# A router's product with the high and low part of its weights side by side, in a decoder layer on one core

## The reference

```python
x = x + attention(layernorm(x))
x = x + convolution(layernorm(x))
h = layernorm(x).reshape(-1, 256)
router_logits = h @ gate_w.T                    # 16 experts
routing_probs = softmax(router_logits)
topk_w, topk_idx = top_k(routing_probs, 4)
topk_w = topk_w / topk_w.sum(-1, keepdims=True)
shared = silu_mul(h @ shared_gate_up.T) @ shared_down.T
shared = shared * sigmoid(h @ shared_gate_vec.T)
x = x + shared + (each expert's output, weighted with topk_w where it is chosen)
```

## Time and profile before

| | |
|---|---|
| median of three runs | 956.32 us |
| the runs | 954.98 to 961.11 us |
| span of the profiled execution | 957.6 us |
| instructions | 19531 |
| mean granted clock of TensorE | 0.989 of 2.4 GHz |
| busy: TensorE, VectorE, GpSimd, ScalarE | 96%, 81%, 53%, 46% |

### The profile page before, as it was taken

How to read it: one execution, slowest core, us unless ns; L and a number is a source line. 1 busy time by engine, 2 the same in 40 slices (tenths; PEclk the granted TensorE clock), 3 DMA queues, 4 the chain that set the end, 5 groups by cost and what they waited for, 6 DMA issues and landing times.

```text
span 957.6 us, 19531 instructions
## 1 busy us (share of the span) xinstructions
PE 919.9 (96%) x6337; PEld 825.6 (86%) x6337; DVE 771.4 (81%) x1704; ACT 439.1 (46%) x1227; POOL 505.0 (53%) x380
## 2 busy tenths in 40 slices
PE   6899999999999999999999999989999999999996
PEld 6789898989899888989888898877887799999985
DVE  6978877977887989877798976765778888888857
ACT  3656745454434654333564333472245444444430
POOL 1453424465453435777453677624626377777760
PEclk9999999999999999999999999998999999999998
DMA  7786389899156952303793231325151277787769
GB/s 267 260 339 238 131 305 388 313 393 364 53 181 246 400 191 105 111 24 117 287 373 115 88 112 48 122 65 237 52 216 69 75 126 130 129 132 129 125 109 314
DMA packets 75586, 179.09 MB, mean 187 GB/s; under 512 B 7777, under 2 KB 42465, under 8 KB 74465
## 3 DMA queue, kind: packets, MB, share of 16 engines
q1 hardware_dynamic: 61040, 158.80, 46.0%
q0 software_dynamic: 14448, 19.05, 12.2%
HBM read 98.35 MB, written 79.47 MB: 186 GB/s over the span
## 4 chain that ended last, share of the span: by engine, by line
PE 76%; DVE 8%; issue 6%; DMA 3%; POOL 3%; ACT 2%; SPq 1%; another core or an unknown queue 0%; DVEq 0%; POOLq 0%; ACTq 0%
PE bank L550 11%; PE bank L552 10%; PE bank L551 10%; PE bank L852 6%; PE bank L630 6%; PE bank L954 3%; POOL xs L1350 3%; PE bank L830 3%; PE bank L616 3%; PE bank L832 3%; PE bank L834 3%; PE bank L656 3%; PE bank L658 2%; PE bank L657 2%; DVE turn L1514 2%
## 5 line engine op out<-in xcount | busy, mean ns | idle before, releaser
L1310 POOL TENSOR_TENSOR z_lo<-prob_t,z_hi 128x512 fp32r<-128x512 f32 x64 | 82.5, 1296 | 191.3 <-ACT z_hi L1197 167.6
L1514 DVE SCALAR_TENSOR_TENSOR turn<-bank,bqk,trig 128x1024 f32<-128x1024 f32 x128 | 160.6, 1277 | 23.3 <-PE bank L552 20.8
L1342 POOL TENSOR_TENSOR rot<-turn 128x512 f32<-128x512 f32 x64 | 101.8, 1591 | 107.4 <-DVE turn L1514 91.9
L1403 POOL DMA_INDIRECT sums<-ysb,token_at x79 | 123.3, 1561 | 57.0 <-DMA sums<-ysb,token_at 26.4
L550 PE MATMUL bank<-xt_hi,w_hi 128*128 128x512 f32 x256 | 105.4, 412 | 3.1 <-DVE xt_lo L1478 1.7
L1183 ACT COPY prob_t<-bank 128x512 f32<-128x512 f32 x64 | 37.5, 586 | 150.9 <-PE bank L616 142.7
L1142 ACT ACTIVATE prob<-prob,negmax 128x128 f32<-128x128 f32 x256 | 99.1, 389 | 2.5 <-DVE negmax L1499 2.4
L552 PE MATMUL bank<-xt_hi,w_lo 128*128 128x512 f32 x256 | 100.0, 391 | 0.0
L551 PE MATMUL bank<-xt_lo,w_hi 128*128 128x512 f32 x256 | 99.7, 390 | 0.0
L1350 POOL DMA_INDIRECT xs<-xh,dest x64 | 71.8, 1122 | 41.9 <-issue 38.3
L1153 ACT COPY v<-bank 128x512 f32<-128x512 f32 x64 | 37.6, 588 | 119.7 <-PE bank L552 118.6
(11 more groups left out here) (201 smaller groups left out, 2663.9 us busy)
## 6 DMA issues: line engine op xcount, KB each, us to landing
xs<-zeros SPq DMA_DIRECT2D x16, 2120.0 KB, 15.6
w_hi<-w_dram SPq DMA_DIRECT2D x24, 768.0 KB, 10.0
w_lo<-w_dram SPq DMA_DIRECT2D x24, 768.0 KB, 9.4
xe_all<-xs SPq DMA_DIRECT2D x79, 132.5 KB
wo_hi<-wo_dram SPq DMA_DIRECT2D x26, 256.0 KB, 9.6
wo_lo<-wo_dram SPq DMA_DIRECT2D x26, 256.0 KB, 11.1
sums<-zeros SPq DMA_DIRECT2D x3, 2176.0 KB, 13.0
raw<-in_wqkv SPq DMA_DIRECT2D x16, 384.0 KB, 4.4
```

Source lines behind the costliest of these rows:

```text
L1342: nc.gpsimd.tensor_tensor(rot[m][1][:], turn[m][1], turn[m][2], ALU.add).then_inc(rot_pool, 1)
L1403: nc.gpsimd.indirect_dma_start(sums_dram[s % SUMS], bass.IndirectOffsetOnAxis(ap=token_at[:, s:s + 1], axis=0), ysb[s % YBUFS][:], None, c ...
L1514: last = nc.vector.scalar_tensor_tensor(turn_all[m][:, 2 * i:2 * i + 2, :], qk_bank[2 * m + i][:].unsqueeze(1).to_broadcast([128, 2, GT]), ...
```

## The change

`gate_hi` and `gate_lo` become the two halves of one tile `gate_both` (36 columns for each half of the features). `token_logits` multiplies the high part and the low part of a block each once with all 36 columns; the sum over both parts and both halves of the features stands in 36 columns of PSUM: what was multiplied with the weights' high part, and beside it what was multiplied with their low part. The product low x low, which was left out before, is now in it. `logits_take` adds the two halves while it moves them to SBUF, with a reduction in place of the copy. A group uses 144 columns of the bank in place of 72. 24 matmuls of 18 columns become 16 of 36. Nothing is moved in any queue.

```diff
         gate = sb("gate", [128, CH, LG])
-        gate_hi = sb("gate_hi", [128, CH, LG], F32R)
-        gate_lo = sb("gate_lo", [128, CH, LG], F32R)
+        gate_both = sb("gate_both", [128, CH, 2 * LG], F32R)
+        gate_hi, gate_lo = gate_both[:, :, 0:LG], gate_both[:, :, LG:2 * LG]
...
                 for b in range(GB):
                     t = slice(b * 128, (b + 1) * 128)
-                    last = product3_at(o[:, b * LG:(b + 1) * LG],
-                                       [(hi[:, c, t], lo[:, c, t], gate_hi[:, c, :], gate_lo[:, c, :])
-                                        for c in range(CH)], b)
+                    for c in range(CH):
+                        for part in (hi, lo):
+                            last = nc.tensor.matmul(o[:, b * 2 * LG:(b + 1) * 2 * LG], part[:, c, t], gate_both[:, c, :],
+                                                    start=(b == 0 and c == 0 and part is hi),
+                                                    stop=(c == CH - 1 and part is lo), skip_group_check=True)
                 last.then_inc(logit_ready, 1)
...
-                    nc.scalar.copy(gate_hi[:], gate[:]).then_inc(gate_hi_done, 1)
+                    nc.scalar.copy(gate_hi, gate[:]).then_inc(gate_hi_done, 1)
...
-                nc.vector.tensor_copy(logit[:, bs, :], bank[:, 0:GB * LG].rearrange("p (b e) -> p b e", b=GB)).then_inc(logit_taken, 1)
+                both = bank[:, 0:GB * 2 * LG].rearrange("p (b h e) -> p b e h", b=GB, h=2)
+                nc.vector.tensor_reduce(logit[:, bs, :], both, AX.X, ALU.add).then_inc(logit_taken, 1)
...
-                    nc.vector.tensor_tensor(gate_lo[:], gate[:], gate_hi[:].bitcast(F32), ALU.subtract).then_inc(gate_lo_done, 1)
+                    nc.vector.tensor_tensor(gate_lo, gate[:], gate_hi.bitcast(F32), ALU.subtract).then_inc(gate_lo_done, 1)
```

## The result

The changed kernel takes 952.98 us (median of 9 executions, 950.46 to 958.89), the kernel before 960.72 in the same series (9 executions, 953.73 to 962.56). The ratio is 0.9938, 95% interval 0.9911 to 0.9966: faster by 0.6%, which is within the 1% called no change. It is taken over all the executions; the two medians alone would give 0.992, since those of nine executions that spread over 8 to 9 us are uncertain by about a microsecond each. The forecast of 950.9 against 956.32 is a ratio of 0.9943.

What follows compares the result with a forecast made beforehand. TensorE, 96% busy, was taken as the bound. -1.78 (groups 0, 1) + 0.12 (group 2) - 0.77 (group 3) - 1.49 - 1.5 (clock) = -5.4 us, from the median of 956.3 to 950.9 us; range 947.0 to 956.5.

Steps and rivals of the forecast that it cites:

- Pitch and run: In each of four places, 16 matmuls start 0.112 us apart; the run takes 1.71 us, 0.89 less.
- The slower rival: Pitch goes with the columns, so each run takes 3.39 us: +2.6 us, 958.9 us; chance 0.05.
- The reduction: VectorE's logits step in each group: reducing 144 values instead of copying 72 adds 0.12 us, between 0.07 and 0.17.
- Groups 0 and 1: Inside the attention loop VectorE keeps up, so the 0.89 us passes twice: -1.78 us.
- The spare: VectorE's waits for TensorE after groups 0 and 1, 2.7 and 1.3 us, exceed 1.01; 0.3 us to spare in group 1.
- second rival: VectorE's queue ends the waits after groups 0 and 1, clock unchanged; only group 3 gains: -0.65, 955.7 us; chance 0.15.
- Group 2: Saved matmul time only lengthens TensorE's idle before the transposes, about 0.9 us; the longer reduction stays: +0.12 us.
- the half: Half of the clock fall behind group 2's run, which cost at most 2.97 us, is spared: -1.5 us.
- Group 3: VectorE waits idle for the logits and the scatter chain follows, so this is the path: -0.89 + 0.12 = -0.77 us.
- The clock: Shorter runs spare the clock fall behind group 0, -1.49 us, and half of group 2's, -1.5 us.
- The first rival: Clock falls stay or as many come elsewhere, so only the work counts: -2.4 us, 953.9 us; chance 0.25.
- One sign that the prediction named for being wrong: Three signs: pitch above 0.14, new TensorE idle in the step after groups 0 and 1, clock falls in stretches without any.

Runs made afterwards that it cites:

- f1: The changed kernel again, unchanged, in the second series of follow-up runs: ratio 0.9938 against the kernel before.
- series 2: Second of three series of follow-up runs on three chips; it holds the kernel before, f1, f2, f3 and f4.
- g1: Changed kernel without the tokens' low part, 8 matmuls of 36 columns in each place: ratio 0.9934 against the kernel before.
- e1: The kernel before, unchanged, run again as a yardstick: ratio 1.0012.
- e4: Kernel before with each matmul of the four runs issued twice, 48 of 18 columns in each: ratio 1.0255.
- e2: Changed kernel with the old 24 matmuls of 18 columns, keeping side-by-side weights and the reduction: ratio 1.0001 against the kernel before.
- f2: Kernel before without the product of tokens' high part and weights' low part, 16 matmuls of 18 columns: ratio 0.9969.
- g2: Kernel before with eight more matmuls of 18 columns in each group, 32 in all, into unread columns: ratio 1.0084.
- f3: Changed kernel with its 16 matmuls reading their 36 columns three times, 108 columns: ratio 0.9965 against the kernel before.
- f4: Kernel before with the 24 matmuls of groups 0 to 2 parted by dense matmuls, group 3 as before: ratio 1.0033.
- e3: Changed kernel with eight more matmuls of 36 columns in each group, 24 in all, into unread columns: ratio 0.9987 against the kernel before.

## Why the prediction was right, and where not

**Pitch and run: right.** 0.112 forecast, 0.1116 measured with 18, 36 and 108 columns; 1.71 us against 1.70. The slower rival, a pitch that goes with the columns, is refuted by the kernel of 108. The cause that the prediction gives, the weight load, was argued from the pitch of 18 and of 256 columns and stays so; no run varies the load. The rule that spoke against the gain, about 25 ns for an isolated matmul of up to 64 columns (the Trainium skill, TensorE: Matmul & The Clock Gate, section Back-to-back issue gap), is not what these streams show, where each matmul has a weight load of its own.

**The reduction: cost too high.** 0.07 us a group instead of 0.12 (301 ns against 0.35 us). I had taken the middle between contiguous and strided; the lower end, 0.30, was right.

**Groups 0 and 1: right.** -0.90 in the table at each, for the forecast of -0.89. The spare came out as described. VectorE's waits for TensorE after, from 339 to 360 (total us, times, longest), to hold against the earlier trace rows:

```profile
DVE turn L1516 <- PE bank L552: 0.7, 1, 0.7
DVE vcs L1566 <- PE bank L648: 0.2, 1, 0.2
```

The 1.8 for the skip product is 0.2 now, the 0.9 for the scores is gone. From 500 to 522 the same two waits stand, the 1.3 has become 0.2. That is the second rival's mechanism come close but not to the point where it decides: with 8 matmuls groups 0 and 1 each gained another 0.90 in the same comparison of starts, and VectorE waited still.

**Group 2: the idle time right, the sum by luck.** TensorE's idle time before the transposes is 1.93 us, 0.77 before: 1.16 longer where 0.9 was said. The saved matmuls bring nothing there. The group still gained 2.50 us in the profile, because its whole clock fall was gone, not the half I had put down. In the repeat of the changed kernel a fall stood there, behind the same idle time of 1.93. So over executions it is there in some and not in others, as the half said, and that the profile of after has none is in part luck. The reason I gave for the half, that TensorE idles there, does not explain the fall of before: it began at 648.97, ahead of the idle time (649.63 to 650.40). It fits the falls of f1 and of the kernel of 8.

**Group 3: right.** -0.66 against -0.77, and VectorE's wait 0.89 shorter.

**The clock: right in size, in part by luck, and one reason wrong.** Forecast -1.49 - 1.5 = -3.0; over all executions of series 2 the clock time fell by 2.67 +- 0.69. Only the profiles tell the places. There the falls of groups 0 and 2 gave -1.49 and -2.50, a microsecond more than forecast, and the new fall at the expert slots took 1.6 back, which no term of the sum foresaw. The first rival, falls that stay or come elsewhere in as many, is refuted for this change by the clock time, and for the runs by the count: 9 of 17 with 24 matmuls, 0 of 16 with 16, 4 of 4 with 32. It was not empty: with 8 matmuls the runs have no fall and the clock time is down by 0.8 +- 0.8 only. One sign that the prediction named for being wrong did come, a fall in a stretch that had none (748.14); the other two did not (the pitch is 0.112, and TensorE is busy for the whole of the windows behind groups 0 and 1). The step that failed is "with each matmul reading twice the columns": 24 of 36 columns fell in two of four runs, 16 of 18 in none, with a clock time as low as that of 36 (6.44 +- 0.59 against 6.11 +- 0.61). The number of matmuls, or the length of the run, does it; the width is not needed. The rule that ties a falling clock to idle gaps between bursts (the Trainium skill, TensorE: Matmul & The Clock Gate, section Why this matters for your kernels) agrees with the falls of f1 and g1 in group 2, behind gaps of 1.93 and 2.83 us, and with those at the slots, and not with the runs: in the windows of e1 and e4 TensorE is busy without a gap and the clock is at 0.50.

**What was given back.** The table's step of +1.82 is the sixteen scatters of group 3, which took longer. (TensorE and VectorE were further ahead by then, at -8.77 us, since the fall of before at 727.47 to 730.89 is absent in after; but the transfers set the path here, and that lead was lost.) The critical chain after (start, length):

```profile
744.18 2.52 DMA xs<-xh,dest
...
748.98 2.00 DMA xe_all<-xs
```

From the first issue to this transfer it is 26.3 us in before (723.24 to 749.55) and 28.1 in after (716.04 to 744.18). The same two lengths return in the other profiles: 26.0 to 26.3 in before, e1, e2, f2, g1 and g2, 28.0 to 28.1 in after, f1, f3, f4, e3 and e4. The two kernels that were profiled twice have the same one both times. Kernels with the side-by-side weights stand in both groups (g1 has the short one), and so do kernels with the separate ones (e4, f4 have the long one), so it is not the edit as such. What sets it I did not find. TensorE waits 4.93 us for the slots, where before it was 1.60 (753.97 to 755.57), and the clock falls at 748.14, still in the wait:

```profile
750.15 0.66 PE L924 MATMUL bank<-ident,xe_all 128*128 128x128 f32 x2 [4.93 <-DMA xe_all<-xs]
```

That is another 1.6 us lost (from -5.4 to -3.8, where the fall ends). This wait is 1.4 to 1.6 us in before, e1 and f2, and none of the three has a fall there; it is 3.5 to 5.0 in the nine other profiles, and all nine have one, of 6.8 us. So a part of the gain goes back where the time spared on TensorE only lengthens a wait for the transfers. Two microseconds came back behind that, mostly later than 896 us, at places that I did not look into; the cause is open. That the profile ends at -5.8 with a forecast of -5.4 is partly chance: for terms of 1.5 to 2 us that the sum did not name cancelled. The mean over executions is the firmer ground: -2.67 of clock and -3.19 +- 0.58 of left time, where the sum had -3.0 and -2.4. The 0.8 more on the left side is 1.4 standard errors, so it may be nothing. The median moved by -5.7 in series 2 (958.99 to 953.31) for -5.4 forecast, half of it work and half of it clock; in the first result it was -7.7, of which the means of the executions show -5.7.

## What to carry to other kernels

Matmuls that bring a weight load of their own and read few columns cost by their number, not by their columns (0.112 us each from 18 to 108 columns here): put what shares a weight side by side and multiply once, and pay the sum of the parts elsewhere. Look at the granted clock behind every stretch of such matmuls, for an engine that is busy without a gap can still lose its clock there; count the falls in several profiles, for one profile has them in some runs and not in others. Where the saved time is turned into a wait, look whether the clock falls behind the longer wait: it can give part of the gain back.

## What the runs showed of the hardware

- The pitch of fp32r matmuls with a weight load of 128 columns each is 0.1116 us at 18, 36 and 108 columns read, and 0.21 at the low clock (342.07, 342.28, 342.50 in the kernel of 32).
- Clock falls begin in or behind an unbroken run of such matmuls in 0 of 16 runs of 16, 9 of 17 runs of 24 and 4 of 4 runs of 32, with TensorE busy throughout. With 32 and 48 all eight begin inside the run and last 6.8 us or more, with 24 one of nine does each (e2's begins inside, before's in group 2 lasts 6.8).
- The 24 other falls, those of the last microseconds aside, each begin in or within 1.5 us behind an idle stretch of TensorE of 0.8 to 5.0 us. Ahead of the expert slots: nine of nine with idle time of 3.5 to 5.0 us, none of three with 1.4 to 1.6.
- The executions' spread is mostly the clock: in the first nine of the changed kernel the clock time has a standard error of 0.75 us, the left time 0.24. Over all kernels the time follows span times (1 - mean granted clock) with a slope of 0.88.
- Sixteen indirect scatters in a row took, from the first start to the last, 26.0 to 26.3 us in six of twelve profiles and 28.0 to 28.1 in the six others. Cause open.
- One GpSimd rotation of 128x512 took 5.20 us in before (at 48.87) and a third of it in after, and the work from there to the first run stood 1.7 us later in before. It goes with the execution and not with the edit: 5.19 to 5.20 us in e1, f1 (the changed kernel) and g2 too. The row of after:

```profile
48.79 1.69 POOL L1344 TENSOR_TENSOR rot<-turn 128x512 f32<-128x512 f32 x1
```
